# Edge-maximum passes: two key one-hots of each step made by ScalarE in place of VectorE

## The chip, the cores and the metric

The kernel runs on one core of a Trainium2 chip. The metric is the device time of one execution in microseconds; the time of a kernel is the median of its runs.

## What is computed

Four graph layers over 3125 nodes of 96 features and 50,000 edges (`src`, `dst`, sorted by `dst`), each behind a layer norm and a relu and each added to its input. The second layer is the one that matters here. It has two rounds of a pooled maximum over incoming edges:

```python
def _sage_pool_layer(x, src, dst, Wp, bp, Ws, Wn, b, n_nodes):
    m = jax.nn.relu(x @ Wp + bp)
    msgs = m[src]
    agg = jax.ops.segment_max(msgs, dst, num_segments=n_nodes)
    agg = jnp.where(jnp.isfinite(agg), agg, 0.0)
    return x @ Ws + agg @ Wn + b
```

The third layer sums `support[edge_col] * edge_weight` by destination, which is a product with a weighted adjacency matrix of source by destination; the fourth propagates 16 times with a normalised adjacency.

## The kernel before

The program runs stages one after the other: a front stage, `build_adjacency`, the attention of the first layer, `first_layer`, `max_pass` (first pooled maximum), `second_layer`, `max_pass` again, `third_layer`, a pass over sums, and the propagation. The change is in `max_pass` (L1794), which runs twice. Each engine has its own instruction list in a `Block`; engines meet only at semaphores (`wait_ge` ahead of an instruction, `then_inc` behind it).

**Two jobs share a pass.** The first is the maximum itself. Edges are taken in NB = 98 blocks of 512. For a near block GpSimd gathers the 512 source rows by four indirect DMAs (`gather`, L1890, issue at L1895) into one of four row buffers; TensorE turns them to feature-by-edge (`turn_rows`, L1919, matmul L1927), VectorE scans them for the running maximum of each destination (`scan`, L2031, L2047), TensorE turns the result back (`turn_back`, L1970, L1977), ScalarE copies it out (`keep_rows`, L2107, L2111) and SP stores it (L2148). For each fourth block (FAR, 22 blocks) nothing is gathered. Instead VectorE makes, for each of T = 25 node tiles, a one-hot of the source ids (`far_hot`, L2054, L2061: 128 x 512 f16) and TensorE multiplies the table tile with it (`add_far`, L1932, two matmuls at L1938). These 25 tiles are spread over the four to five steps before the far block's scan.

**The second job**, in the same steps, is a quarter of the weighted adjacency matrix's work for the third layer. There are PARTS = 25 * 4 = 100 steps of it in each pass. A step n has m = 3, 3, 3 or 4 windows (`STEP_WINS`). For each window TensorE multiplies a 128 x 128 matrix of edge weights by destination lane with a 128 x 125 one-hot of keys (`lay_out`, L1942, L1957). The lane matrices come from VectorE (`lanes_of` L2009, `weigh` L2026). The key one-hots come from VectorE (`keys_of`, L2013, compare at L2017, one instruction a window). In every second step from 4 on (`firsts`), GpSimd makes the first of them (`first_key`, L1883, compare at L1888), three steps ahead. Then ScalarE copies the sum to f16 (`high_part`, L2091, L2097), VectorE takes the rest (`low_part`, L2050, L2052), TensorE turns six or seven tiles (`turn_piece`, L1961, L1967), ScalarE keeps them (`keep_piece`, L2099, L2104), and SP stores 2 x 400 KB every fourth step (L2126).

**The order of the work is written out by hand.** In step m:

- TensorE: `turn_back(m-6)`, a far tile, `turn_rows(m-4)`, two far tiles, `lay_out(m)`, the remaining far tiles, `turn_piece`.
- VectorE: `scan(m-5)`, `low_part(m-1)`, a far one-hot for step m+1, `lanes_of(m+1)`, a far one-hot, `weigh(m+1)`, two far one-hots, `keys_of(m+1)`, the remaining far one-hots.
- ScalarE: `keep_rows(m-6)`, `high_part(m)`, `keep_piece`.
- GpSimd: two gathers of block m, a first key for step m+3 if that is one of `firsts`, two more gathers.

VectorE's key one-hots alternate between two buffers, GpSimd's first keys between four. A gather waits for the gather of the same quarter in the near block before (the fourth before it) to have landed, and for the row buffer to be free (TensorE's turn of four near blocks earlier). Far one-hots have six buffers. The last far tile is made in step 91; the steps behind that have none.

Elsewhere, in `build_adjacency`, ScalarE already makes some key one-hots by two ACTIVATEs: an Abs of (key - column) at L1350 and a Relu of (1 - distance) at L1355.

Of the kernel before, what the change touches and what calls it, by code (L numbers as in the profile page):

```python
# [19 lines left out]
F16 = mybir.dt.float16  # L20
I32 = mybir.dt.int32
ALU = mybir.AluOpType
ACT = mybir.ActivationFunctionType
# [8 lines left out]
P = 128  # L32
# [22 lines left out]
QUARTER = 4  # L55
HALF = P // 2
FEW = 5
FEW_KEYS = FEW * T
# [1735 lines left out]
def max_pass(nc, c, name, table_dram, src_rows, same_dram, tables, rows_dram, weights_dram, part, adj, numbers, minus, ids_dram, away_dram=None):  # L1794
# [8 lines left out]
    PARTS = T * QUARTER  # L1803
    WIDEST = max(STEP_WINS)
    assert RING == QUARTER and sum(PIECES) == T and NB <= PARTS <= P
    with stack() as ctx:
# [19 lines left out]
        key_hot = [sb(f"key_hot{i}", [P, WIDEST, FEW_KEYS + 3], F16) for i in range(2)]  # L1826
        first_key_hot = [sb(f"first_key_hot{i}", [P, FEW_KEYS + 3], F16) for i in range(FIRSTS)]
        first_key_made = sem("first_key_made")
        firsts = [k for k in range(PARTS) if k >= AHEAD and (k - AHEAD) % 2 == 1]
        firsts_until = lambda n: sum(k < n for k in firsts)  # L1830
        keys, lanes, weights = pass_tables(tables)
# [86 lines left out]
        def _(pe):  # L1918
# [23 lines left out]
            def lay_out(n):  # L1942
                if n >= 2:

                    pe.wait_ge(lo_kept, n - 1)
                pe.wait_ge(lanes_ready, n + 1)
                for w in range(STEP_WINS[n % QUARTER]):
                    m = window_dst(WIN_AT[n % QUARTER] + w)
                    by_pool = w == 0 and n in firsts
                    hot_of = first_key_hot[firsts_until(n) % FIRSTS][:, 0:FEW_KEYS] if by_pool else key_hot[n % 2][:, w, 0:FEW_KEYS]  # L1950
                    keys_of = hot_of.rearrange("p (k d) -> p k d", k=T)[:, :, 0:m]
                    if by_pool:
                        pe.wait_ge(first_key_made, firsts_until(n) + 1)
                    else:
                        pe.wait_ge(hots_ready, first_win[n] + w + 1 - firsts_until(n + 1))
                    for h in range(2):
                        mm = nc.tensor.matmul(by_source(n)[:, :, FEW * w:FEW * w + m], lanes_by_weight(n)[:, h, w, :], keys_of,  # L1957
                                              start=w == 0 and h == 0, stop=h == 1, skip_group_check=True)
                mm.then_inc(hots_used, 1)
# [41 lines left out]
        def _(dve):  # L2001
# [11 lines left out]
            def keys_of(n):  # L2013
                first, m = first_win[n], STEP_WINS[n % QUARTER]

                for w in range(int(n in firsts), m):
                    nc.vector.tensor_scalar(key_hot[n % 2][:, w, 0:FEW_KEYS], columns, keys[:, first + w:first + w + 1], None, ALU.is_equal).then_inc(hots_ready, 1)  # L2017

            def weigh(n):
# [70 lines left out]
        def _(act):  # L2090
# [8 lines left out]
            def keep_piece(i, q):  # L2099
                act.wait_ge(piece_turned, 4 * i + q + 1)  # L2100
                if q == 0 and i >= 2:

                    act.wait_ge(rows_stored[i % 2], 32 * (i // 2))
                nc.scalar.activation(rows_w[i % 2][:, first_tile[q]:first_tile[q] + PIECES[q], :].rearrange("d k p -> d (k p)"),  # L2104
                                     piece_ps[:, 0:PIECES[q] * P], ACT.Copy).then_inc(piece_kept, 1)

            def keep_rows(n):  # L2107
                act.wait_ge(back, n + 1)
                if n >= OUTS:
                    act.wait_ge(written[n % OUTS], 16 * (n // OUTS))  # L2110
                nc.scalar.activation(out[n % OUTS][:, :, :].rearrange("p j d -> p (j d)"), back_ps[:, 0:4 * D], ACT.Copy).then_inc(kept, 1)  # L2111

            for m in range(NB + BACK):
                if m >= BACK:
                    keep_rows(m - BACK)
                if m < PARTS:
                    high_part(m)
                for i, q in pieces_of(m):
                    keep_piece(i, q)

        @block.sync
        def _(sp):
# [553 lines left out]
```

## Time and profile before

| | us |
|---|---|
| median of 3 runs (lowest to highest) | 2730.33 (2725.48 to 2733.41) |
| the profiled execution | 2735.16 |
| its span in the profile | 2733.4 |
| PE (TensorE matmul) busy | 2470.2 (90%) |
| PEld (weight load) busy | 1996.7 (73%) |
| DVE (VectorE) busy | 1901.7 (70%) |
| ACT (ScalarE) busy | 1059.6 (39%) |
| POOL (GpSimd) busy | 1207.4 (44%) |

The profile is of one execution. Busy time is the union of an engine's instructions; issuing, branches and semaphore instructions are not in it. The first edge-maximum pass lies at 663 to about 1150 us of the span, the second at 1211 to about 1710. The 1.7 us between the profiled execution and its span lie around the program.

### The profile page before, as it was taken

To read this page: it belongs to the slowest core of one execution; us is meant where nothing else is said; L and a number is where in the kernel's file an instruction comes from. 1 tells how busy PE (TensorE), PEld (TensorE's weight loads), DVE (VectorE), ACT (ScalarE), POOL (GpSimd) and SP (SyncE) were. 2 spreads that over 40 slices of the span, in tenths; PEclk is the share of its full clock that TensorE was granted. 3 is DMA by queue.
4 is the path that set the end of the run, shared out by engine and by line. 5 is a ranking of instruction groups with operands and counts; after the bars stand their busy time and mean duration, and the time that the engine had idled before them with its cause. 6 is when DMAs were issued, how large, how long until landed. Compare 5 with 4: busy or idle time off the path is not lost. (4 is left out here: it accounts for less than half of the span.)

```text
span 2733.4 us, 72547 instructions
## 1 busy us (share of the span) xinstructions
PE 2470.2 (90%) x29368; PEld 1996.7 (73%) x29368; DVE 1901.7 (70%) x5337; ACT 1059.6 (39%) x2385; POOL 1207.4 (44%) x1471
## 2 busy tenths in 40 slices
PE   6998999995999999679999995589899999999999
PEld 4666777774666666456666664478899999999998
DVE  6997999997999999459999994400544444444444
ACT  5997888884333333223333332300411111111110
POOL 4006999992777777557777775310000000000000
PEclk8558999997999999689999996589999999999999
DMA  5103000004555555525555555289000000000000
GB/s 169 43 2 104 12 13 12 13 11 128 137 148 138 144 135 149 142 81 134 148 134 153 146 136 165 80 290 315 2 2 2 2 2 2 2 2 2 2 2 19
DMA packets 147300, 226.90 MB, mean 83 GB/s; under 512 B 55184, under 2 KB 113259, under 8 KB 146290
## 3 DMA queue, kind: packets, MB, share of 16 engines
q1 hardware_dynamic: 121502, 185.74, 22.7%
q0 software_dynamic: 21920, 35.15, 6.5%
q8 instruction: 237, 3.88, 0.6%
q10 hardware_dynamic: 3540, 1.30, 0.2%
q14 instruction: 101, 0.83, 0.1%
HBM read 121.74 MB, written 100.35 MB: 81 GB/s over the span
## 5 line engine op out<-in xcount | busy, mean ns | idle before, releaser
L1895 POOL DMA_INDIRECT max_row<-table,max_src_rows x608 | 660.3, 1086 | 265.1 <-issue 155.1
L1938 PE MATMUL max_far<-adj 128*96 128x512 f16 x2200 | 566.5, 383 | 5.4 <-DVE adj L2061 3.9
L1758 POOL TENSOR_SCALAR e<-e 128x512 f32<-128x512 f32 (+1 forms) x625 | 366.8, 606 | 178.1 <-ACT e L1746 161.0
L1772 DVE TENSOR_TENSOR e<-e,a_ps 128x1024 f32<-128x1024 f32 (+1 forms) x313 | 372.4, 1195 | 33.1 <-PE a_ps L1684 13.0
L2402 PE MATMUL prop<-g,adj 128*128 128x192 f16 x4608 | 386.4, 247 | 9.4 <-DVE g L2476 9.4
L2402 PEld LDWEIGHTS prop<-g,adj 128*128 128x128 f16 x4608 | 379.9, 98 | 14.2 <-issue 9.2
L2061 DVE TENSOR_SCALAR adj<-adj,node_numbers 128x512 f16<-128x512 f16 x1100 | 368.5, 359 | 25.4 <-PE max_far L1938 20.9
L2402 PE MATMUL prop<-weights_then_states,adj 128*128 128x192 f16 x4608 | 384.3, 246 | 0.0
L2402 PEld LDWEIGHTS prop<-weights_then_states,adj 128*128 128x128 f16 x4608 | 378.9, 98 | 3.7 <-issue 2.5
L1746 ACT ACTIVATE e<-s_ps 128x512 f32<-128x512 f32 (+1 forms) x625 | 335.6, 585 | 60.6 <-PE o_ps L1696 35.6
L1938 PEld LDWEIGHTS max_far<-adj 128*96 128x96 f16 x2200 | 250.1, 128 | 129.9 <-DVE adj L2061 21.0
L2510 DVE SCALAR_TENSOR_TENSOR support_parts<-prop,coef,weights_then_states 128x96 f32<-128x96 f32 x384 | 120.6, 314 | 303.7 <-PE prop L2402 225.8
L2097 ACT ACTIVATE max_strip<-max_strip_ps 128x375 f16<-128x375 f32 x200 | 105.8, 529 | 401.9 <-PE max_strip_ps L1957 401.7
L2047 DVE TENSOR_TENSOR_SCAN max_run<-max_same,max_run,max_col 96x512 f32<-96x512 f16 x152 | 192.5, 1266 | 36.2 <-PE max_col L1927 20.7
L1696 PE MATMUL o_ps<-e,v_all 128*25 128x128 f32 (+1 forms) x5000 | 197.2, 276 | 4.6 <-DVE e L1772 2.1
L1674 PE MATMUL s_ps<-q_tile,k_all 96*128 96x128 f16 (+1 forms) x2500 | 190.5, 219 | 5.3 <-DMA k_all<-qk_dram 5.3
L1927 PE MATMUL max_col<-ident,max_row 128*96 128x128 f16 x1216 | 122.9, 231 | 73.3 <-DMA max_row<-table,max_src_rows 71.0
L1927 PEld LDWEIGHTS max_col<-ident,max_row 128*96 128x96 f16 x1216 | 98.3, 128 | 118.8 <-DMA max_row<-table,max_src_rows 87.9
L2570 ACT ACTIVATE weights_then_states<-support_parts 128x96 f16<-128x96 f32 (+1 forms) x200 | 56.5, 283 | 328.3 <-DVE support_parts L2512 328.3
L2570 ACT ACTIVATE g<-support_parts 128x96 f16<-128x96 f32 (+1 forms) x175 | 49.5, 283 | 298.2 <-DVE support_parts L2512 298.2
L1674 PEld LDWEIGHTS s_ps<-q_tile,k_all 96*128 96x128 f16 x2500 | 154.3, 98 | 6.1 <-DMA k_all<-qk_dram 5.8
L1696 PEld LDWEIGHTS o_ps<-e,v_all 128*25 128x25 f32 x5000 | 112.6, 103 | 43.7 <-DVE e L1772 21.6
(288 smaller groups left out, 3485.9 us busy)
## 6 DMA issues: line engine op xcount, KB each, us to landing
weights_then_states<-weights SPq DMA_DIRECT2D x100, 400.0 KB, 4.8
weights<-max_rows_w SPq DMA_DIRECT2D x52, 400.0 KB
rows_dram<-max_out SPq DMA_DIRECT2D x100, 192.0 KB, 1.9
weights<-adj SPq DMA_DIRECT2D x48, 400.0 KB
max_same<-same_dram SPq DMA_DIRECT2D x196, 96.0 KB, 3.2
rows_dram<-adj SPq DMA_DIRECT2D x96, 192.0 KB, 3.7
max_row<-table,max_src_rows POOLq DMA_INDIRECT x608
adj<-ids_dram SPq DMA_DIRECT2D x44, 128.0 KB, 3.7
```

Source lines behind the costliest of these rows:

```text
L1674: mm = nc.tensor.matmul(s_ps[u % S_RINGS][:, hd * w:(hd + 1) * w], k_st[:, hd, t * P:(t + 1) * P], q_st[:, row % 2, hd, 0:w], start=True, ...
L1696: mm = nc.tensor.matmul(o_ps[row % 2][hd * VW:hd * VW + DH + 1, 0:w], v_all[:, t, hd, :], e_tile(u)[:, hd * w:(hd + 1) * w], start=t == 0, ...
L1746: nc.scalar.activation(e_tile(u), s_ps[u % S_RINGS][:, 0:HEADS * width(row)], ACT.Exp).then_inc(exped, 1)
L1758: nc.gpsimd.tensor_scalar(e_tile(u), e_tile(u), math.exp(10.0), math.exp(-10.0), ALU.min, ALU.max).then_inc(clipped, 1)
L1772: nc.vector.tensor_tensor(tile, tile, a.unsqueeze(2).to_broadcast([P, n, HEADS, w]), ALU.mult).then_inc(weighted, 1)
L1895: nc.gpsimd.indirect_dma_start(row[i % RING][:, j, :], None, table_dram, bass.IndirectOffsetOnAxis(ap=src_rows[:, 4 * n + j:4 * n + j + 1] ...
L1927: mm = nc.tensor.matmul(col_ps[i % 2][0:D, j * P:(j + 1) * P], row_parts[i % RING][:, j, a, :], c.ident16[:, :], start=a == 0, stop=a == 1 ...
L1938: mm = nc.tensor.matmul(far_ps[j % 2][0:D, :], parts[:, k, a, :], hot[(T * j + k) % HOTS], start=k == a == 0, stop=k == T - 1 and a == 1)
L2047: nc.vector.tensor_tensor_scan(run[n % 2][:, :], same[n % SAME][:, :], cols[0:D, :], run[1 - n % 2][:, BLK - 1:BLK], ALU.mult, ALU.max).th ...
L2061: nc.vector.tensor_scalar(hot[i % HOTS], ids[j % 2], numbers[:, k:k + 1], None, ALU.is_equal).then_inc(hot_made, 1)
L2402: return nc.tensor.matmul(sums(step, t), adj[:, k, t * P:(t + 1) * P], states[:, k, :], start=start and t % 2 == 0, stop=k == END - 1 and ...
L2510: nc.vector.scalar_tensor_tensor(part[rows, t % 2, :], total[rows, D:2 * D], coef[rows, t:t + 1], base[rows, t, :], ALU.mult, ALU.add).the ...
```

## The change

In each of the 100 steps of a pass, the last two key one-hots (BY_SCALAR = 2) are made by ScalarE. For windows at, at+1 with at = m - 2 it computes the absolute distance of each column to the key (`measure`, two Abs instructions of 128 x 125), and then one Relu of (1 - distance) over both, which is 1 where they are equal and 0 elsewhere (`last_keys`, 128 x 2 x 125). `keys_of` on VectorE stops two windows earlier, and `lay_out` waits for `last_keys_made` ahead of those two windows. ScalarE makes the keys of step m+2 in step m: the Abs pair between `keep_rows` and `high_part`, the Relu at the step's end. Its Relu waits for its own two Abs and for TensorE to have used the buffer two steps before. Steps 0 and 1 are made ahead of the loop.

```diff
@@ -1826,6 +1826,9 @@
         key_hot = [sb(f"key_hot{i}", [P, WIDEST, FEW_KEYS + 3], F16) for i in range(2)]
         first_key_hot = [sb(f"first_key_hot{i}", [P, FEW_KEYS + 3], F16) for i in range(FIRSTS)]
         first_key_made = sem("first_key_made")
+        BY_SCALAR = 2
+        key_distance = sb("key_distance", [P, 2, BY_SCALAR, FEW_KEYS + 3], F16)
+        distance_made, last_keys_made = sem("distance_made"), sem("last_keys_made")
         firsts = [k for k in range(PARTS) if k >= AHEAD and (k - AHEAD) % 2 == 1]
         firsts_until = lambda n: sum(k < n for k in firsts)
         keys, lanes, weights = pass_tables(tables)
@@ -1951,8 +1954,10 @@
                     keys_of = hot_of.rearrange("p (k d) -> p k d", k=T)[:, :, 0:m]
                     if by_pool:
                         pe.wait_ge(first_key_made, firsts_until(n) + 1)
+                    elif w < STEP_WINS[n % QUARTER] - BY_SCALAR:
+                        pe.wait_ge(hots_ready, first_win[n] - BY_SCALAR * n + w + 1 - firsts_until(n + 1))
                     else:
-                        pe.wait_ge(hots_ready, first_win[n] + w + 1 - firsts_until(n + 1))
+                        pe.wait_ge(last_keys_made, n + 1)
                     for h in range(2):
                         mm = nc.tensor.matmul(by_source(n)[:, :, FEW * w:FEW * w + m], lanes_by_weight(n)[:, h, w, :], keys_of,
                                               start=w == 0 and h == 0, stop=h == 1, skip_group_check=True)
@@ -2013,7 +2018,7 @@
             def keys_of(n):
                 first, m = first_win[n], STEP_WINS[n % QUARTER]
 
-                for w in range(int(n in firsts), m):
+                for w in range(int(n in firsts), m - BY_SCALAR):
                     nc.vector.tensor_scalar(key_hot[n % 2][:, w, 0:FEW_KEYS], columns, keys[:, first + w:first + w + 1], None, ALU.is_equal).then_inc(hots_ready, 1)
 
             def weigh(n):
@@ -2110,13 +2115,35 @@
                     act.wait_ge(written[n % OUTS], 16 * (n // OUTS))
                 nc.scalar.activation(out[n % OUTS][:, :, :].rearrange("p j d -> p (j d)"), back_ps[:, 0:4 * D], ACT.Copy).then_inc(kept, 1)
 
+            def measure(n):
+                at = STEP_WINS[n % QUARTER] - BY_SCALAR
+                for w in range(BY_SCALAR):
+                    s = first_win[n] + at + w
+                    nc.scalar.activation(key_distance[:, n % 2, w, 0:FEW_KEYS], columns, ACT.Abs, scale=-1.0, bias=keys[:, s:s + 1]).then_inc(distance_made, 1)
+
+            def last_keys(n):
+                at = STEP_WINS[n % QUARTER] - BY_SCALAR
+                if n >= 2:
+
+                    act.wait_ge(hots_used, n - 1)
+                act.wait_ge(distance_made, BY_SCALAR * (n + 1))
+                nc.scalar.activation(key_hot[n % 2][:, at:at + BY_SCALAR, 0:FEW_KEYS], key_distance[:, n % 2, :, 0:FEW_KEYS], ACT.Relu, scale=-1.0,
+                                     bias=c.ones[:, 0:1]).then_inc(last_keys_made, 1)
+
+            for n in range(2):
+                measure(n)
+                last_keys(n)
             for m in range(NB + BACK):
                 if m >= BACK:
                     keep_rows(m - BACK)
+                if m + 2 < PARTS:
+                    measure(m + 2)
                 if m < PARTS:
                     high_part(m)
                 for i, q in pieces_of(m):
                     keep_piece(i, q)
+                if m + 2 < PARTS:
+                    last_keys(m + 2)
 
         @block.sync
         def _(sp):
```

## Rows read from the trace of the kernel before

**Rows 1.** Page, the chain of work that ended last, by engine.

```profile
PE 33%; DMA 1%; DVE 1%; ACT 0%; issue 0%; DVEq 0%
```

**Rows 2.** Busy time by stretch: long part and tail, both passes, one slice.

```profile
663.00:1103.00 440.00, 403.92 (x3177) 281.33 (x3177) 426.62 (x1185) 158.74 (x273) 344.11 (x322) 0.99 0.55 139
1103.00:1144.00 41.00, 25.83 (x180) 20.84 (x181) 21.12 (x41) 12.61 (x21) 28.85 (x31) 0.58 0.52 129
...
sum 968.00, PE 863.54 PEld 605.39 DVE 897.19 ACT 344.29 POOL 742.47; mean PE 215.88 PEld 151.35 DVE 224.30 ACT 86.07 POOL 185.62
...
1448.00:1488.00 40.00, 38.16 (x301) 25.76 (x299) 40.00 (x114) 14.12 (x26) 30.90 (x31) 1.00 0.56 144
```

**Rows 3.** Sources L1895 and L1888: ns min/median/max; idle us, times.

```profile
L1895 POOL DMA_INDIRECT max_row<-table,max_src_rows x608: 940/1028/2447, 663.6 to 1690.3; - x152
...
  issue: 155.1, 538
  DMA max_row<-table,max_src_rows: 55.1, 67
...
  PE max_col L1927: 0.6, 1
...
L1888 POOL TENSOR_SCALAR max_first_key_hot<-adj,max_tables x96: 625/852/1969, 671.5 to 1678.1; 128x125 f16<-128x125 f16 x96
```

**Rows 4.** Groups of instructions on GpSimd, whole trace: busy us, mean ns.

```profile
L1895 POOL DMA_INDIRECT max_row<-table,max_src_rows x608 | 660.3, 1086 | 265.1 <-issue 155.1 <-DMA max_row<-table,max_src_rows 55.1 <-POOLq L106 54.3
...
L1888 POOL TENSOR_SCALAR max_first_key_hot<-adj,max_tables 128x125 f16<-128x125 f16 x96 | 82.2, 856 | 3.1
```

**Rows 5.** Timeline, pass 1: first gather, last gather, last turn of rows.

```profile
663.60 1.31 POOL L1895 DMA_INDIRECT max_row<-table,max_src_rows  x1 [39.83 <-POOLq L106]
...
1139.58 0.95 POOL L1895 DMA_INDIRECT max_row<-table,max_src_rows  x1 [0.30 <-issue]
...
1143.64 0.45 PE L1927 MATMUL max_col<-ident,max_row 128*96 128x128 f16 x2 [0.84 <-DMA max_row<-table,max_src_rows]
```

**Rows 6.** Source L1927 (turning rows), idle before it: us, times.

```profile
  DMA max_row<-table,max_src_rows: 158.9, 202
```

**Rows 7.** Gathers (L1895) alone, tail of pass 1.

```profile
1103.00:1144.00 41.00, 26.94 (x28) 0.58 0.52 129
```

**Rows 8.** Timeline around one long gather, pass 1: start us, us.

```profile
862.95 1.95 POOL L1895 DMA_INDIRECT max_row<-table,max_src_rows  x1 [0.17 <-issue]
863.03 0.60 DVE L2061 TENSOR_SCALAR adj<-adj,node_numbers 128x512 f16<-128x512 f16 x2
...
863.55 0.44 DVE L2017 TENSOR_SCALAR max_key_hot<-adj,max_tables 128x125 f16<-128x125 f16 x2
...
863.91 0.86 DVE L2061 TENSOR_SCALAR adj<-adj,node_numbers 128x512 f16<-128x512 f16 x3
...
865.54 0.49 ACT L2097 ACTIVATE max_strip<-max_strip_ps 128x375 f16<-128x375 f32 x1 [1.02 <-PE max_strip_ps L1957]
```

**Rows 9.** Groups of instructions on VectorE: busy us, mean ns.

```profile
L2061 DVE TENSOR_SCALAR adj<-adj,node_numbers 128x512 f16<-128x512 f16 x1100 | 368.5, 359 | 25.4 <-PE max_far L1938 20.9 <-DMA adj<-ids_dram 4.1
...
L2017 DVE TENSOR_SCALAR max_key_hot<-adj,max_tables 128x125 f16<-128x125 f16 x554 | 116.9, 291 | 0.0
```

**Rows 10.** Sources L2097 (idle before it) and L2104 (ns min/median/max).

```profile
  PE max_strip_ps L1957: 401.7, 198
...
L2104 ACT ACTIVATE adj<-max_piece x96: 811/811/918, 693.4 to 1684.9; 128x768 f16<-128x768 f16 x72, 128x896 f16<-128x896 f16 x24
```

**Rows 11.** Timeline of ScalarE in the adjacency stage: start us, us.

```profile
60.94 0.40 ACT L1350 ACTIVATE key_distance<-iota,tables 128x125 f16<-128x125 f16 x1 [4.98 <-PEq L818]
61.37 0.40 ACT L1355 ACTIVATE key_hot<-key_distance,ones 128x125 f16<-128x125 f16 x1
61.68 0.39 ACT L1350 ACTIVATE key_distance<-iota,tables 128x125 f16<-128x125 f16 x1
```

**Rows 12.** One of the three table loads on ScalarE.

```profile
L258 ACT ACT_TABLE_LOAD x1 | 1.3, 1283 | 9.2 <-DVE l_mean_var L325 9.2
```

## The prediction

> **What bounds the kernel now.** I start with the chain of work that ended last. It lies almost wholly in the propagation at the end [rows 1] and says nothing about the two edge-maximum passes, so the passes have to be read from their own stretches. A pass has a long part with far blocks and a short tail without them; in the long part the busy times are about 97% for VectorE, 92% for TensorE, 36% for ScalarE and 78% for GpSimd [rows 2]. By those shares VectorE is the bound, and in one slice of 40 us it is busy for all of it [rows 2]. I do not believe that reading, for three reasons.
>
> First, GpSimd is not idle in the rest of its time. Of 608 gathers 538 have only the issue gap ahead of them, 0.29 us on average, and 67 waited for the landing of an earlier gather; for a consumer (the ring of row buffers, freed by TensorE) it waited once, 0.6 us [rows 3]. An engine held back by a slower one would wait for it, and GpSimd does not.
>
> Second, its own chain adds up to the pass. In one pass 304 gathers at their shortest, 0.94 us [rows 3], with 0.30 us of issue are 377 us; 48 first keys at their shortest, 0.63 us [rows 3], are 25 us once the shorter gap after each (0.17 us, before the gather of rows 8) is set against the small one ahead. The mean gather is 1.086 us, so stretching costs 304 x 0.146 = 44 us, and 48 keys at 0.856 us are stretched by 11 us [rows 4]. Half of the 55.1 us of landing waits, less 0.30 us for each of 33 places, is 18 us [rows 3]. That is 475 us; from the first gather of pass 1 (663.60) to the end of its last (1140.53) it is 477 us [rows 5].
>
> Third, the pass ends on it: the last turns of rows wait for gathers [rows 5], and over both passes TensorE's matmuls and weight loads were held up 202 times by a gathered row [rows 6]. So the pace is **GpSimd's, stretched by something**, with VectorE only a few per cent behind.
>
> What stretches it? In the tail, where VectorE is half idle, gathers take 0.96 us (26.94 us for 28) [rows 7]. One row shows the mechanism: a gather started at 862.95 lasts 1.95 us. Over it lies an unbroken run of VectorE's f16 SBUF-to-SBUF compares: two far one-hots, two key one-hots, three far one-hots, 863.03 to 864.77; the gather ends 0.13 us after the run [rows 8]. The last gather of the pass, with VectorE idle, takes 0.95 us [rows 5]. The long run, far, keys, far, comes once in a step, and the keys are its middle. The Trainium skill (SBUF — State Buffer, section "Who interferes with whom") says why: such a `tensor_scalar` may take a port pair that GpSimd shares, while ScalarE waits for nobody and blocks nobody. By that rule the work moved to ScalarE stops costing GpSimd anything; this trace agrees for VectorE's side.
>
> **The change part by part.** *Removed from VectorE:* two of three or four key compares in each of 100 steps of two passes, 400 of 554. They are 116.9 us busy [rows 9], 0.21 us each, so 84 us, 0.42 us a step. In the even steps from 4 on, where GpSimd makes the first key of three, VectorE makes none at all. On the path this is worth nothing by itself: cover is GpSimd's chain. If that cover were absent, it would be the whole 84 us.
>
> *Less stretching of GpSimd.* Both passes have 608 x (1.086 - 0.94) = 89 us on gathers and 96 x (0.856 - 0.63) = 22 us on first keys [rows 3, 4], 111 us in all. Which share goes? Lower bound: by all of VectorE's work, 84 of 897 us [rows 2], 9%, 10 us. By the compares that form the runs, 84 of 368.5 + 116.9 us [rows 9], 17%, 19 us. Upper bound: the run of rows 8 loses its 0.4 us of about 1.7; if the delay goes with the square of the run's length, 1 - (1.3/1.7)^2 = 42% or 46 us. I take 19 us, because the long waits sit on that kind of instruction. Part comes back: 67 gathers waited for the landing of the fourth gather before [rows 3], and what GpSimd gained over the three between is lost there, 201 of 608 gathers, so up to a third. I take off 4 us. Term: **-15 us**, between -46 and 0 (a gain of zero if VectorE's far compares merely slide under other gathers).
>
> *Added to ScalarE:* in each step two Abs of 125 columns, 0.40 us each, and one Relu over 250. The same pair runs elsewhere in the kernel: Abs to Relu 0.43 us apart, Relu to Abs 0.31 us, 0.40 us for a Relu of 125 columns [rows 11]. 128 more columns cost 0.107 us in the copy of a piece (0.811 against 0.918) [rows 10], so the Relu takes 0.50 us and a step 0.31 + 0.43 + 0.50 = 1.24 us. ScalarE goes from 1.7 us a step to 2.9 us of 4.8. It is hidden in its own wait: 198 waits for the strip sums, 401.7 us, 2.0 us each [rows 10]. Where the wait is short, as at 865.54, it holds 1.02 of the 1.24 us [rows 8] and the high part comes some 0.2 us late. Behind it in VectorE's queue stand the low part, the far one-hots and the lanes of the next step, and TensorE waits for those; VectorE has 0.42 us a step in hand, so I cost it at nothing. The new wait of the Relu on the two Abs holds the next step's copy of rows back by under 0.5 us, and the store on SP behind it; TensorE needs that bank free only one step later. The wait for the one-hots' last user is always met, since the high part ahead of it waited for the same matmuls. Bounds: 0 to +1.24 us a step.
>
> The Trainium skill (ScalarE: Activation LUTs, section "Rules for kernel authors") speaks against the move: relu and the like belong on VectorE. The rows agree on the price, 1.24 against 0.42 us a step; the rule would decide if ScalarE bounded the pass, which is the last rival.
>
> *The keys' way to TensorE:* the keys of step m+2 are made in ScalarE's step m and used two steps later, with a step in hand. At the start of a pass, ScalarE needs 1.24 us from the block's start, while GpSimd's first gather only starts at 663.60 [rows 5]: nothing. *Tables:* Abs, Relu and Copy ran before without a load of their own; the trace has three table loads in all, 1.28 us each [rows 12]: nothing, at worst 2.6 us.
>
> **Sum.** The profiled execution took 2735.16 us around a span of 2733.4; minus 15 is 2720. That execution is 4.8 us above the median of the runs, 2730.33, so the forecast for the median is **2715 us**.
>
> **Rivals.** *A, VectorE is the pace after all.* For it: its slices at 100% [rows 2]. Against: GpSimd never waits for anyone. It would give -84 us, 2646, and nearly all stretching of GpSimd would have to go as well. Chance 0.08.
>
> *B, no change.* The stretching stays, because five or six far compares a step still make a run and the freed time only shifts them, or landings take the gain back. Short stretches outside the long run speak for it. It gives 0, within 8 us, 2730. Chance 0.22.
>
> *C, slower: ScalarE's high part comes late.* Place: the copy of rows, then two Abs, stand ahead of the high part; VectorE's low part waits for it and holds the far one-hots back, and TensorE then falls behind GpSimd's pace. It decides from the point where lateness exceeds VectorE's 0.42 us plus its reserve of some 0.1 us a step. If the whole 1.24 us showed in a quarter of the 176 steps with far work, 44 x (1.24 - 0.52) = +32 us, 2762. Against: the wait it fills is 2.0 us on average. Chance 0.12.
>
> **Chances.** My forecast, a gain of 8 to 46 us, 0.58; A 0.08; B 0.22; C 0.12. A measurement of this kernel tells about 0.3%, 8 us, from no change. Faster: 0.58 + 0.08 = 0.66; same 0.22; slower 0.12. The range leaves out A and C: from 2730 - 40 to just above the median, 2690 to 2735.
>
> **What would show it.** Right: GpSimd's mean gather falls from 1.086 us to about 1.05 and its gaps stay at 0.30 us with no wait for TensorE; VectorE's busy time in a pass falls by 42 us and its waits for TensorE's row sums grow; the low part waits little for the high part. Wrong, toward A: GpSimd's gaps had hidden a wait and the gathers shorten to near 0.94 us. Toward B: mean gather unchanged or landing waits up by what it gained. Toward C: long waits of VectorE's low part for ScalarE, TensorE's for far one-hots, and GpSimd waiting for TensorE's turns. Two more table loads would be my error on tables.

## Result, and the profile after

The change is **slower by 0.4%**: 2740.7 us at the median of 18 runs (2725.67 to 2752.56) against 2727.84 us (2714.1 to 2736.46) for 18 runs of the kernel before on the same chip, ratio 1.004, 95% interval 1.0027 to 1.0053. Ratios here and below leave out executions that fell into a slower state of the chip, are given with an interval, and can differ from the quotient of the two medians (1.0047 here). I had given 2715 us, a range up to 2735, and 0.12 for slower.

The two profiled executions hide this: before took 2735.16 us, above its median, after 2737.28, below its own, so they stand 2 us apart where the medians stand 12.9 apart. Not too much may be read from one pair, and further down I pool several profiles.

The page of the kernel after, section 1, busy time by engine:

```profile
PE 2458.7 (90%) x29368; PEld 1997.5 (73%) x29368; DVE 1846.5 (67%) x4937; ACT 1251.2 (46%) x2985; POOL 1195.1 (44%) x1471
```

VectorE's was 1901.7 us before, ScalarE's 1059.6, GpSimd's 1207.4. Groups of instructions on GpSimd, after; they answer to [rows 4]:

```profile
L1898 POOL DMA_INDIRECT max_row<-table,max_src_rows x608 | 642.1, 1056 | 276.6 <-issue 151.7 <-DMA max_row<-table,max_src_rows 69.1 <-POOLq L106 54.0
...
L1891 POOL TENSOR_SCALAR max_first_key_hot<-adj,max_tables 128x125 f16<-128x125 f16 x96 | 89.0, 927 | 3.3
```

The gathers shrank by 18.2 us, as I had forecast; but the first keys grew by 6.8 us, where I had them shrinking, and the landing waits by 14.0. I call GpSimd's chain the busy and idle time of both rows together; it was 660.3 + 82.2 + 265.1 + 3.1 = 1010.7 us before and is 642.1 + 89.0 + 276.6 + 3.3 = 1011.0 after. Nothing is left of the gain.

The source of the gathers, after: idle time before them in us, and times [rows 3]:

```profile
  issue: 151.7, 539
  DMA max_row<-table,max_src_rows: 69.1, 62
  POOLq L106: 54.0, 2
  PE max_col L1930: 1.7, 5
```

The gaps are still the issue gap (151.7 / 539 = 0.28 us), and GpSimd waits for TensorE only 5 times. Groups on VectorE and on ScalarE, after [rows 9, 10]:

```profile
L2066 DVE TENSOR_SCALAR adj<-adj,node_numbers 128x512 f16<-128x512 f16 x1100 | 374.6, 362 | 71.6 <-PE max_far L1941 60.5 <-DMA adj<-ids_dram 4.8
L2057 DVE TENSOR_TENSOR max_strip<-max_strip_ps,max_strip 128x375 f16<-128x375 f32 x200 | 109.1, 546 | 10.1 <-ACT max_strip L2102 10.1
L2022 DVE TENSOR_SCALAR max_key_hot<-adj,max_tables 128x125 f16<-128x125 f16 x154 | 38.2, 288 | 0.0
```

```profile
L2122 ACT ACTIVATE max_key_distance<-adj,max_tables 128x125 f16<-128x125 f16 x400 | 137.0, 397 | 10.2 <-PEq L106 10.2
L2102 ACT ACTIVATE max_strip<-max_strip_ps 128x375 f16<-128x375 f32 x200 | 105.5, 528 | 208.0 <-PE max_strip_ps L1962 205.4
L2130 ACT ACTIVATE max_key_hot<-max_key_distance,ones 128x250 f16<-128x250 f16 x200 | 99.4, 497 | 0.1
```

ScalarE's additions came out as costed: 0.40 us for an Abs, 0.50 for the Relu, paid out of its wait for the strip sums (401.7 to 205.4 us). VectorE's low part waits 10.1 us for the high part, 5.7 before. VectorE's own relief is smaller than costed: 1901.7 - 1846.5 = 55 us, not 84. The keys' own row falls by 78.7 us (the remaining keys take 0.25 us each instead of 0.21), and the far compares take 6 us more. The rest is not split here in full; part of it is time that an instruction shares with its neighbour, which the total counts once ([rows 8]: the compares from 863.03 end 0.08 us after the keys behind them start). An instruction inside a run is cheaper than one alone: in the timeline after, four far compares in a row take 1.12 us, 0.28 each, and one alone 0.34.

```profile
868.78 0.34 DVE L2066 TENSOR_SCALAR adj<-adj,node_numbers 128x512 f16<-128x512 f16 x1
869.04 0.54 DVE L2031 TENSOR_TENSOR max_lane_w<-adj,max_tables 128x768 f16<-128x768 f16 x1
869.51 1.12 DVE L2066 TENSOR_SCALAR adj<-adj,node_numbers 128x512 f16<-128x512 f16 x4
...
873.08 0.68 DVE L2031 TENSOR_TENSOR adj<-adj,max_tables 128x1024 f16<-128x1024 f16 x1
```

GpSimd's timeline of the same place, after (start, length in us, in brackets the idle time before):

```profile
869.23 1.53 POOL L1898 DMA_INDIRECT max_row<-table,max_src_rows  x1 [1.06 <-DMA max_row<-table,max_src_rows]
871.06 1.05 POOL L1898 DMA_INDIRECT max_row<-table,max_src_rows  x1 [0.30 <-issue]
872.14 1.15 POOL L1891 TENSOR_SCALAR max_first_key_hot<-adj,max_tables 128x125 f16<-128x125 f16 x1
873.46 1.46 POOL L1898 DMA_INDIRECT max_row<-table,max_src_rows  x1 [0.17 <-issue]
```

One step shows all three. The gather at 869.23 waits 1.06 us for a landing, and then lies under the weighing (L2031, 869.04) and the run of four compares, and is stretched to 1.53 us; the first key at 872.14 takes 1.15 us where its shortest is 0.63, beside two far compares, the lanes and the weighing.

### The profile page after: what moved, and what is told of

Its sections match the earlier page's. It is cut to its first block and busy times, and to the rows that moved or that the text cites. A ratio compares the mean times of both kernels' runs of the same rounds, so it can differ in the third digit from the quotient of the medians.

```text
span 2735.6 us, 72943 instructions
## 1 busy us (share of the span) xinstructions
PE 2458.7 (90%) x29368; PEld 1997.5 (73%) x29368; DVE 1846.5 (67%) x4937; ACT 1251.2 (46%) x2985; POOL 1195.1 (44%) x1471
## 5 line engine op out<-in xcount | busy, mean ns | idle before, releaser
L1898 POOL DMA_INDIRECT max_row<-table,max_src_rows x608 | 642.1, 1056 | 276.6 <-issue 151.7
L2066 DVE TENSOR_SCALAR adj<-adj,node_numbers 128x512 f16<-128x512 f16 x1100 | 374.6, 362 | 71.6 <-PE max_far L1941 60.5
L2102 ACT ACTIVATE max_strip<-max_strip_ps 128x375 f16<-128x375 f32 x200 | 105.5, 528 | 208.0 <-PE max_strip_ps L1962 205.4
L1696 PEld LDWEIGHTS o_ps<-e,v_all 128*25 128x25 f32 x5000 | 112.9, 104 | 43.3 <-DVE e L1772 19.8
```

The costliest lines, as they stand in the source:

```text
L1696: mm = nc.tensor.matmul(o_ps[row % 2][hd * VW:hd * VW + DH + 1, 0:w], v_all[:, t, hd, :], e_tile(u)[:, hd * w:(hd + 1) * w], start=t == 0, ...
L1898: nc.gpsimd.indirect_dma_start(row[i % RING][:, j, :], None, table_dram, bass.IndirectOffsetOnAxis(ap=src_rows[:, 4 * n + j:4 * n + j + 1] ...
L2066: nc.vector.tensor_scalar(hot[i % HOTS], ids[j % 2], numbers[:, k:k + 1], None, ALU.is_equal).then_inc(hot_made, 1)
```

## The experiments

Open after the result: does the loss come from what ScalarE got, or from what VectorE lost? Does it come through the landing waits, and are those made by the stores of tiles that share the DMA engines, or by the single semaphore of each quarter? Is GpSimd's chain the pace at all? All ratios are against the kernel before on the same chip, with 95% intervals. The runs were taken in five groups, each on one chip and each with the kernel before beside it. In the first, fourth and fifth group the kernel before took 2731.92 to 2736.44 us, in the second and third, on two other chips, 2770.19 and 2759.69. This turned out to matter.

**Relief alone.** From before: VectorE makes its keys of a step but the last two, and nobody makes those. TensorE still does all its products, with what the buffers hold, and waits for all of VectorE's keys of the step at once, where before it waited window by window.

```diff
-                for w in range(int(n in firsts), m):
+                for w in by_vector(n):
...
+        LEFT = 2
+        by_vector = lambda n: list(range(WIDEST)) if n < 2 else list(range(int(n in firsts), STEP_WINS[n % QUARTER] - LEFT))
```

> VectorE makes two key one-hots fewer in each step and nobody makes them in its place (from step 2 on TensorE multiplies with one-hots left over from the first steps, so the adjacency part of the output is not computed); ScalarE is as before. Theory S (the change's loss comes from ScalarE's added 1.24 us a step, and the relief of VectorE is worth what was forecast): 10 to 15 us faster than before, GpSimd's gathers at about 1.055 us and landing waits near the 55 us of before. Theory L (the relief itself is given back, because a GpSimd that is stretched less runs into the landing of its own earlier gathers): within 5 us of before, gathers at 1.055 us, landing waits near 69 us.

2748.34 us, ratio 1.0037 (1.0016 to 1.0059). Two instructions a step less on a 97% busy engine, nothing added anywhere, and the kernel is as slow as after.

**ScalarE's work alone.** Before, with the Abs pair and the Relu of every step added, written to a tile of their own; VectorE still makes all its keys.

```diff
+                nc.scalar.activation(key_distance[:, n % 2, :, 0:FEW_KEYS], key_distance[:, n % 2, :, 0:FEW_KEYS], ACT.Relu, scale=-1.0,
+                                     bias=c.ones[:, 0:1]).then_inc(last_keys_made, 1)
```

> The kernel before, VectorE making all its key one-hots, and ScalarE doing the Abs pair and the Relu of the change on top, at the same places, into a tile that nobody reads. Theory S: slower than before by 20 to 25 us (the 11 us lost and the gain forecast). Theory L: within 3 us of before, since ScalarE's instructions fit into its waits. Either way GpSimd's mean gather stays at 1.086 us.

2730.65 us, 0.9985 (0.9967 to 1.0002): 1.24 us a step on ScalarE costs nothing that can be seen. Its groups show the same 0.397 and 0.497 us as after:

```profile
L2120 ACT ACTIVATE max_key_distance<-adj,max_tables 128x125 f16<-128x125 f16 x400 | 137.1, 397 | 9.6 <-PEq L106 9.6
...
L2128 ACT ACTIVATE max_key_distance<-max_key_distance,ones 128x250 f16<-128x250 f16 x200 | 99.5, 497 | 0.1
```

These two runs split the change: the relief alone is as slow as the whole change (1.0037 and 1.004), and no loss comes from the ScalarE work alone.

**The Abs pair last.** After, with the measure moved behind the pieces, so that the high part is not held back by 0.7 us.

```diff
-                if m + 2 < PARTS:
-                    measure(m + 2)
                 if m < PARTS:
...
                 if m + 2 < PARTS:
+                    measure(m + 2)
                     last_keys(m + 2)
```

> The changed kernel with the Abs pair moved from ahead of the high part to the end of ScalarE's step, just before the Relu. Theory S: the high part is no longer late, so 10 to 25 us faster than the changed kernel, that is 0 to 15 us faster than before, and VectorE's waits of the low part for ScalarE fall from 10 us to about 5. Theory L: like the changed kernel, within 4 us.

2733.14 us, 0.9965 (0.9938 to 0.9992). ScalarE does the same work in another place and there is no loss (after itself was not timed beside it, and the 12 times are spread more widely than the others, 2705.96 to 2747.04). By itself this would speak for a late high part; but the relief alone loses without any Abs, so a shift of the engines' work against each other fits too. Its profiled execution (2740.97) lies above its median and shows no cleaner chain than after's.

**No first keys.** After, and GpSimd makes none; VectorE makes those 48 a pass.

```diff
-        firsts = [k for k in range(PARTS) if k >= AHEAD and (k - AHEAD) % 2 == 1]
+        firsts = []
```

> The changed kernel with GpSimd's 96 first keys given back to VectorE (ScalarE keeps the last two of each step): GpSimd only gathers. If GpSimd's own chain is the pace, it loses 48 x (0.93 - 0.13) = 38 us a pass, 76 us in both, until VectorE or TensorE is the pace: 30 to 70 us faster than before. If something else sets the pace (VectorE with TensorE, or ScalarE's high part), within 10 us of the changed kernel.

2652.67 us, 0.9692 (0.9667 to 0.9718); repeated in the fourth group, on another chip,

> e4_no_first_keys again. If GpSimd's chain is the pace on this chip too: 75 to 95 us faster than before. If this chip is of the kind where GpSimd waits for TensorE's turns: the 70 us that GpSimd saves turn into that wait, and it is between 10 us faster and 20 us slower than before.

2652.81 us, 0.9699 (0.9676 to 0.9721). GpSimd's groups and a stretch of each pass (busy time and count of PE, PEld, DVE, ACT, POOL):

```profile
L1898 POOL DMA_INDIRECT max_row<-table,max_src_rows x608 | 652.5, 1073 | 275.4 <-issue 155.4 <-DMA max_row<-table,max_src_rows 63.0 <-POOLq L106 54.3
```

```profile
700.00:900.00 200.00, 198.66 (x1608) 142.57 (x1607) 195.75 (x524) 123.38 (x274) 149.38 (x140) 1.00 0.63 155
1250.00:1450.00 200.00, 199.76 (x1623) 143.57 (x1622) 199.15 (x533) 124.91 (x278) 149.24 (x139) 1.00 0.65 160
```

The chain is now 652.5 + 275.4 = 927.9 us, 83 less than before, and the time falls by 84, more than the 70 I had expected at most. GpSimd's chain is the pace here: what is taken off it comes off the time, while VectorE gets work back. In these stretches TensorE and VectorE are both close to full, at 98% or more. The same two stretches of before had 184.5 and 184.9 us of TensorE.

**Stores of the tiles moved out of the passes** (all 24 behind the last step, with the wait that guarded them gone), from before and from after.

```diff
-                if m % QUARTER == QUARTER - 1 and QUARTER <= m < PARTS:
-                    store_tile(m // QUARTER - 1)
...
-            store_tile(T - 1)
+            for i in range(T):
+                store_tile(i)
```

> The kernel before with the 24 stores of weight tiles inside each pass (2 x 400 KB every fourth step) moved behind the pass's last step; what they store is then mostly of the last two tiles, so the adjacency part of the output is not the reference's. It is the base for the next run. Theory L (GpSimd waits for the landing of its own earlier gathers because the stores' bursts delay them): landing waits beyond the usual gap fall from 40 us to under 10 us, and GpSimd's two chains shorten from 956 to about 925 us; the stores behind the passes add their own time to the whole. Rival (landings are late for another reason): 40 us stays.

> The same move of the stores in the changed kernel; to be compared with the run before this one. Theory L: without bursts the change has nothing to give its gain back to but the first keys; gathers' stretch 15 to 18 us less, first keys' 7 to 10 us more, so 5 to 10 us faster than the run before this one (against 11 us slower with the bursts). Rival (the give-back has nothing to do with the bursts): 8 to 13 us slower than the run before this one, as with the bursts.

2913.92 us, 1.052 (1.0492 to 1.0548), and 2925.51 us, 1.0549 (1.0524 to 1.0574). The stores behind the end cost far more than they could free, so the pair is read only against each other: after is still 11.6 us slower. But this is not the same loss. On this chip the first keys do not grow with the relief (73.3 and 72.2 us), landing waits are 8.0 and 6.9 us in all, and what grows is GpSimd's wait for TensorE, from 52.5 to 74.5 us. Whether the stores' bursts have a part in the loss of the first chips is left open by this pair.

**No first keys, from before,** on the same chip.

```diff
-        firsts = [k for k in range(PARTS) if k >= AHEAD and (k - AHEAD) % 2 == 1]
+        firsts = []
```

> The kernel before with GpSimd's 96 first keys given back to VectorE, which then makes all 650 key one-hots. Beside e4_no_first_keys it shows what the change does where GpSimd has no first keys. If VectorE is then the pace here, some 20 to 40 us faster than before only, and the two keys on ScalarE are worth 40 to 60 us there. If GpSimd's gathers are still the pace, 2650 to 2665 us, and the change is worth nothing there either.

2785.87 us, 1.0063 (1.0042 to 1.0085). I had expected a gain. The source of its gathers ("remote" is a wait whose releaser the profile can't name):

```profile
  issue: 149.8, 486
  PE max_col L1927: 110.5, 47
  POOLq L106: 54.3, 2
  remote: 39.6, 45
  DMA max_row<-table,max_src_rows: 16.3, 28
```

GpSimd waits 110.5 us for TensorE's turns here, and little for landings. VectorE has all keys in this kernel, which could explain it; the runs below without that trait, with two semaphores, are slower than before as well.

**Stores two steps apart** (no first keys, the halves of a tile stored in two steps):

```diff
-                    store_tile(m // QUARTER - 1)
+                    store_tile(m // QUARTER - 1, (0,))
+                if m % QUARTER == 1 and 2 * QUARTER <= m < PARTS + QUARTER:
+                    store_tile(m // QUARTER - 2, (1,))
```

> e4_no_first_keys with the two 400 KB stores of a tile issued two steps apart in place of back to back. Theory L: each gather meets at most half a burst, landing waits beyond the gap fall from 37 us to under 15 us, and the time from 2653 us to about 2630 to 2640 us. Rival: the same bytes delay the gathers as much in two parts, within 5 us of e4_no_first_keys.

2810.69 us, 1.012 (1.0072 to 1.0168). Its profiled execution took 2829.14 us, far from its median, and the kernel without the split was not timed on this chip, so I draw nothing from it: inconclusive.

**Two semaphores to a quarter.** The gather of step n then waits for the landing two near steps back instead of one, so that it hardly ever waits for one.

```diff
-                if i >= 1:
-                    pool.wait_ge(gathered[j], 16 * i)
+                if i >= 2:
+                    pool.wait_ge(gathered[j][i % 2], 16 * (i // 2))
```

> The kernel before with two semaphores for each quarter of a block in place of one, so that a gather waits for the landing of the eighth gather before it and not of the fourth. It is the base for the next run. If the landing waits are on the path (40 us of GpSimd's two chains before), they go, and the kernel is 25 to 40 us faster than before. If they are only where GpSimd would have waited for something else, within 5 us.

> The same two semaphores in the changed kernel; to be compared with the run before this one. Theory L (the relief of VectorE shortens the gathers, and the waits for the fourth gather's landing eat it): with those waits gone the gathers' 15 to 18 us less stay, against 7 to 10 us more on the first keys, so 3 to 12 us faster than the run before this one. Theory P (the relief locks VectorE's and GpSimd's order of work together so that stretching moves rather than goes, and the landing waits are no cause): 5 to 15 us slower than the run before this one, as without the two semaphores.

> The changed kernel without GpSimd's first keys (VectorE makes them, ScalarE keeps the last two) and with the two semaphores. GpSimd's chain of a pass is then 304 x 1.24 us and 40 us of stretching, about 417 us, and VectorE, 98% busy without the two semaphores, is the next bound: 85 to 100 us faster than before, no more than 15 us beyond e4_no_first_keys, which was 84 us faster than the kernel before.

> The run before this one with ScalarE's Abs pair at the end of its step. With GpSimd no longer the pace, the high part's lateness could show: up to 10 us faster than the run before this one if it does, within 4 us if it does not.

From before: 2756.9 us, 0.9991 (0.9977 to 1.0005). From after: 2759.32, 0.9999 (0.9985 to 1.0013). Without first keys: 2773.75, 1.0052 (1.0034 to 1.007). The same with the Abs pair last: 2777.36, 1.0042 (1.002 to 1.0065). Landing waits are 1.7 to 5.4 us in these profiles, but before gains nothing where I had expected 25 to 40 us, after is level, and the kernel without first keys, 3% faster in the first group, is slower. On this chip too the first keys do not grow with the relief: 74.3 us from before, 75.0 from after. GpSimd's gathers in the third of them:

```profile
L1898 POOL DMA_INDIRECT max_row<-table,max_src_rows x608 | 630.6, 1037 | 406.4 <-issue 149.8 <-PE max_col L1931 126.7 <-remote 69.0
```

A stretch of the second pass in the same run, to be read beside that of the kernel without first keys above:

```profile
1250.00:1450.00 200.00, 179.85 (x1382) 122.02 (x1379) 171.47 (x447) 106.63 (x236) 127.93 (x124) 0.96 0.55 136
```

Either the deeper wait changes what bounds the kernel, or this chip is not like the first. So the plain kernels were run again, on a further chip.

**Repeats,** without a further edit: before, after, relief alone, and no first keys (above).

> The kernel before, unchanged, for a profile of it beside the next three on one chip. Within 3 us of before. If this chip is of the kind of the first two (before at 2727 and 2736 us), GpSimd waits for TensorE for under 3 us; if of the kind of the other two (2770 and 2760 us), it waits for the turns of rows for 20 us or more.

> The changed kernel, unchanged. If the loss is the same on every chip: 6 to 16 us slower than before. If it hangs on the chip: within 4 us where GpSimd waits for TensorE (there the relief of VectorE could even help), 6 to 16 us slower where it does not.

> e1_relief_only again. Where GpSimd is the pace: 5 to 15 us slower than before, gathers' stretch down by 15 us, first keys' up by 10, landing waits up by 14. If the loss of e1_relief_only was of that chip alone: within 5 us of before.

2733.41 us, 0.999 (0.9972 to 1.0008); 2739.01, 1.0017 (0.9999 to 1.0035); 2741.06, 1.0013 (0.9996 to 1.003); and 0.9699 for the kernel without first keys. The last brings back the 3%. By the time of the kernel before, the chips are of two kinds. On those where it takes 2732 to 2736 us GpSimd hardly waits for TensorE (17 times, 5.4 us, in the repeat without first keys); in every profile from those where it takes 2760 to 2770 it does. But none of the latter is of a plain kernel: every run there had a further edit or other keys, so chip and kernel are not told apart. The loss of after and of the relief is smaller here, 0.1 to 0.2%, and both intervals include 1.

**Relief, padded.** The relief alone, and VectorE gets as many microseconds back as a `tensor_reduce` over a table, ahead of its keys. It forms no run with the compares.

```diff
+                if n >= 2:
+                    nc.vector.tensor_reduce(pad_max[:, 0:1], c.iota16[:, 0:350], AX.X, ALU.max)
```

> e1_relief_only with one reduction of 350 f16 columns into one (about 0.42 us) on VectorE in each step, in place of the two key compares that it leaves out: VectorE is as long busy as before, but with an instruction that reads one SBUF tile and writes next to nothing. Theory P (the loss is VectorE's timing: relieved by 0.4 us a step, it falls into another place against GpSimd's instructions, which lengthens the first keys and the gather of the landing wait): first keys' stretch back near 21 us, landing waits near 40 us, gathers' stretch at or below the 75 us of e1_relief_only, and 5 to 20 us faster than before. Rival (the loss is something else that leaving out two keys does): within 5 us of e1_relief_only, 4 to 10 us slower than before.

2727.52 us, 0.9986 (0.9964 to 1.0007). Groups of VectorE and GpSimd:

```profile
L2021 DVE TENSOR_REDUCE max_pad_max<-iota 128x1 f16<-128x350 f16 x196 | 99.1, 506 | 0.0
```

```profile
L1899 POOL DMA_INDIRECT max_row<-table,max_src_rows x608 | 661.5, 1088 | 262.3 <-issue 154.2 <-POOLq L106 54.9 <-DMA max_row<-table,max_src_rows 51.0
...
L1892 POOL TENSOR_SCALAR max_first_key_hot<-adj,max_tables 128x125 f16<-128x125 f16 x96 | 78.3, 815 | 3.2
```

With the length of VectorE's step given back, and with other work, every quantity returns to that of before: keys 78.3 us, landing waits 51.0, and the gathers' stretch as well (mean 1.088). So the loss does not come from the absence of the two keys as such; it goes with the length of VectorE's step, and by it with the place of its instructions against GpSimd's. I had expected the gathers to keep their shorter mean and the kernel to be 5 to 20 us faster than before; it is level with it. That the added instruction itself stretches the gathers no run here excludes. In the tail of a pass one gather took 1.33 us with only the weighing (L2032) and that reduction over it:

```profile
1116.72 1.33 POOL L1899 DMA_INDIRECT max_row<-table,max_src_rows  x1 [0.30 <-issue]
1116.67 0.56 DVE L2032 TENSOR_TENSOR max_lane_w<-adj,max_tables 128x768 f16<-128x768 f16 x1
1117.14 0.52 DVE L2021 TENSOR_REDUCE max_pad_max<-iota 128x1 f16<-128x350 f16 x1
```

**The first key ahead of the gather that waits.** After, with GpSimd's first key of a step moved ahead of gather 0 instead of behind gather 1, to fill the landing wait.

```diff
+                if n + AHEAD in firsts:
+                    first_key(n + AHEAD)
                 if n in nth:
...
                     gather(n, 1)
-                if n + AHEAD in firsts:
-                    first_key(n + AHEAD)
```

> The changed kernel with GpSimd's first key ahead of the first gather of its step in place of behind the second. The landing wait of 37 us sits almost wholly ahead of the first gather of each step 3 mod 4, which has no key between it and the gather it waits for. With the key there the time is filled. If the landing waits are real waits for a landing at a time of its own: they fall from about 50 us to under 20 us, and the kernel is 15 to 35 us faster than before. If they only stand for lost phase: the time is that of the changed kernel within 5 us.

2706.97 us, 0.9907 (0.9882 to 0.9932).

```profile
L1898 POOL DMA_INDIRECT max_row<-table,max_src_rows x608 | 638.9, 1051 | 251.7 <-issue 159.9 <-POOLq L106 55.6 <-DMA max_row<-table,max_src_rows 36.3
...
L1891 POOL TENSOR_SCALAR max_first_key_hot<-adj,max_tables 128x125 f16<-128x125 f16 x96 | 83.1, 866 | 3.1
```

The landing waits fall from 69.1 to 36.3 us and the keys by 6: the chain is 976.8 us, 34 less than after's or before's (1011.0, 1010.7), the time 25 less than before's. Both places of the loss can be won back, and more.

## Why the prediction was wrong

**What held.** On the first kind of chip GpSimd's chain is the pace of both passes, and VectorE at 97% is not: 83 us off the chain gave 84 us, while a relief of VectorE by 55 us gave none. Rival A is out. The 1.24 us a step on ScalarE is hidden in its wait, at 0.397 and 0.497 us an instruction, and there was no further table load; so rival C, which had the right sign, had the wrong mechanism. The gathers did shorten, to the 1.05 us I had named, and GpSimd still hardly waited for its consumer (1.7 us, 5 times).

**The step that failed** is "Less stretching of GpSimd", in its two halves: the first keys' stretch, which I let fall with that of the gathers as one average share, and the 4 us given back to landing waits. The term was forecast at -15 us and came out at +10.8. The profiles pooled, in us over both passes, each from the two GpSimd rows of its trace:

| | gathers | first keys | idle | of it landing | sum |
|---|---|---|---|---|---|
| before | 660.3 | 82.2 | 268.2 | 55.1 | 1010.7 |
| before, repeat | 654.7 | 81.0 | 268.5 | 56.6 | 1004.2 |
| ScalarE's work alone | 653.9 | 80.8 | 267.1 | 54.2 | 1001.8 |
| relief, padded | 661.5 | 78.3 | 265.5 | 51.0 | 1005.3 |
| after | 642.1 | 89.0 | 279.9 | 69.1 | 1011.0 |
| after, repeat | 646.0 | 94.5 | 275.0 | 63.2 | 1015.5 |
| relief alone | 646.0 | 92.6 | 282.8 | 70.4 | 1021.4 |
| relief, repeat | 646.9 | 93.6 | 276.9 | 66.5 | 1017.4 |
| Abs pair last | 653.0 | 90.1 | 270.2 | 57.6 | 1013.3 |

The first four (VectorE's step at its old length) have a mean of 1005.5 us, the next four (relieved) 1016.3; the kernel with its Abs pair last lies between in every column, from a profile some 8 us above its median, and is in neither mean. Against the first four the relieved kernels have 12.3 us less in the gathers, 11.8 us more in the first keys, and 11.3 us more in the idle time, where the landing waits alone are up by 13.1. The balance is +10.8 us. The executions from which the sums come are 10.2 us apart in the mean (2742.2 and 2731.9), so the chain accounts for the loss in them. After's median was 12.9 us above before's in the first comparison and 5.6 in the repeat. The sums of one kernel's two profiles differ by 4 to 7 us, so one pair of them could not have shown it.

By my working the gathers should have given about 15 of the 19 us (their share of the stretch was 89 of 111); they gave 12. The first keys should have given 4 and took 12: a term with the wrong sign. The landing waits should have taken 4 and took 13. Each of the two missed terms alone nearly eats the gain.

**The mechanism.** Shown: relieving VectorE makes it wait longer for TensorE's far sums (60.5 us after, 20.9 before; 67.5 in the relief alone, 6.8 padded), and relieved and relieved-and-padded differ in nothing but one VectorE instruction of 0.51 us a step, and all three columns change over. Seen in the traces, not separately tested: which instruction now lies over which. Laying the start and end times of VectorE's instructions over GpSimd's, for both passes:

| us of overlap | first keys under the weighing | gathers under the weighing | gathers under far compares | gathers under key compares |
|---|---|---|---|---|
| old length: before, repeat, ScalarE's work alone | 10.3, 9.5, 6.1 | 85.1, 89.1, 90.6 | 260.3, 253.9, 259.7 | 125.8, 127.7, 120.2 |
| relief, padded | 3.6 | 93.8 | 258.4 | 34.6 |
| relieved: after, repeat, relief alone, repeat | 19.3, 21.5, 23.2, 21.1 | 74.1, 73.7, 70.2, 72.3 | 257.8, 257.9, 260.3, 260.7 | 38.5, 37.7, 43.3, 43.0 |

The weighing has moved from the gathers to the first keys (the example at 872.14). The far compares lie over the gathers as long as ever. So what shortened the gathers is open between two things that go together here: the key compares that are gone and the weighing that moved away. The padded kernel has as few key compares over its gathers as the relieved ones, and its gathers are as long as before.

The Trainium skill (SBUF — State Buffer, section "Who interferes with whom") has a sentence that bears on the first keys: "A DVE instruction with two SBUF inputs contends with a GpSimd instruction that reads SBUF". The weighing is such an instruction and the first key such a reader; the rows agree: the first keys lie under the weighing for 19 to 23 us where it was 4 to 10, and take 12 us more. The same section has `tensor_reduce` never contending on trn2; in the padded kernel the gathers are nevertheless back at 1.088 us on average. If that rule holds here, the stretch came from the place of the other instructions, not from the added one; no run here tests it.

**Rival B** named part of this, that landings could take the gain back, and would have been nearest. What none of my cases held is that the sum could go beyond zero by it. I had bounded the term at 0 from above "if far compares merely slide under other gathers", and a slide has no such bound: it can fall on a dearer place as well as on a cheaper one.

**Open.** Why two kinds of chip behave differently. On the one GpSimd is the pace and freeing it pays 3%; on the other it waits for TensorE, and kernels with the same edit, but from before or with one edit more, are 0.4 to 1.2% slower. The profiles hold one lead: in 1250 to 1450 us of the span TensorE's granted clock was 0.99 or 1.00 in before, after and the kernel without first keys on the first kind, and 0.96 in that of the third run with two semaphores on the other, where it fell for a few us at a time to the lower of its two levels (1.2 of 2.4 GHz) and a far matmul (L1942) took up to 0.65 us instead of 0.38. But TensorE is also less busy there (179.85 us against 199.76) and did 15% fewer matmuls (1382 against 1623), which a clock 4% lower does not cover; what came first no run here tells. Why the loss of the relief is 0.4% in two comparisons and 0.1 to 0.2% in two others. Why a gather that is awaited lands late enough to stall: the stores' part in it was not tested on a chip that shows the wait. And why moving the Abs pair helps: in its profile the first keys lie under the weighing for 19.4 us, as in the relieved kernels.

## What to carry to other kernels

Look for the engine that never waits for its consumers; that one was the pace here, however full its neighbour. Look again on another chip: on two of them GpSimd did wait. Then take work off that engine itself (no first keys, -3.1%) or reorder it to fill its own waits (-0.9%), rather than relieve the neighbour that disturbs it. And a relief isn't one-sided: it moves the relieved engine's instructions against the bound one's, so cost it place by place, or give it a range that reaches past zero on both sides.

## What the runs showed that I had not expected

Taking two instructions a step from a 97% busy engine made the kernel slower (1.0037, and 1.0013 with an interval that includes 1 in the repeat), and putting a useless one of 0.51 us back made it as fast as before (0.9986). One edit, GpSimd's first keys to VectorE, was 3.1 and 3.0% faster on two chips, and 0.6% slower (from before, without ScalarE's keys) or 0.5% slower (with them, and two semaphores to a quarter) on two others; the kernel differs there as well as the chip. On the first kind it is the best version found, 2652.67 us against 2736.44 before.
